# Gated cross-attention and FFN on one core: other orders at the start and in the last three attention pairs, four places for V

## What is computed

```python
q = (layernorm(x) @ Wq)          # 32 heads
k, v = ctx @ Wk, ctx @ Wv        # 8 heads, each used by 4 query heads
q, k = rope(q), rope(k)          # cos/sin rows gathered by position_ids
p = softmax(where(mask == 0, -1e9, q @ k.T / sqrt(128)))
x = x + tanh(g_xattn) * ((p @ v) @ Wo)
x12 = layernorm(x) @ w12.T + b12
x = x + tanh(g_ffn) * ((silu(x12[..., :512]) * x12[..., 512:]) @ w3.T + b3)
```

## Time and profile before

| | |
|---|---|
| median of 3 runs | 682.74 us (681.73 to 683.15) |
| the profiled execution | 682.45 us, of which the span (first to last instruction) is 680.6 us |
| PE busy | 663.5 us, 97% of the span, 3352 matmuls |
| PE weight loads busy | 555.4 us, 82% |
| DVE, POOL, ACT busy | 485.0, 385.3, 321.9 us |
| mean granted TensorE clock | 0.997 of full |
| chain that ended last | PE 86%, DVE 5%, POOL 3%, ACT 2% |

### The profile page before, as it was taken

One profiled execution on the slowest core, in us unless ns is written; L12 is line 12 of the kernel. 1 busy time (PEld: TensorE's weight loads), 2 busy tenths in 40 slices (PEclk: granted clock), 3 DMA queues, 4 the chain that ended last, 5 costly groups with the idle time before them and its releaser, 6 DMA issues.

```text
span 680.6 us, 11325 instructions
## 1 busy us (share of the span) xinstructions
PE 663.5 (97%) x3352; PEld 555.4 (82%) x3352; DVE 485.0 (71%) x1223; ACT 321.9 (47%) x903; POOL 385.3 (57%) x323
## 2 busy tenths in 40 slices
PE   7999999999999999999999999999999998999998
PEld 6777888778888888888888888888888886778886
DVE  2788575887777777777777777777777776774433
ACT  4343722554544545445445454454454536766210
POOL 5546766886556666665566666655666655531000
PEclk8999999999999999999999999999999999999999
DMA  9977894232122131213212121221210042000002
GB/s 304 311 242 232 272 309 155 90 97 93 58 83 93 35 105 33 92 31 108 91 32 94 47 92 31 93 70 69 77 33 31 32 155 79 0 1 1 1 31 93
DMA packets 62157, 66.34 MB, mean 97 GB/s; under 512 B 5920, under 2 KB 43808, under 8 KB 62112
## 3 DMA queue, kind: packets, MB, share of 16 engines
q1 hardware_dynamic: 60688, 64.77, 29.4%
q0 software_dynamic: 384, 1.05, 0.5%
q10 hardware_dynamic: 1040, 0.00, 0.1%
HBM read 46.93 MB, written 18.87 MB: 97 GB/s over the span
## 4 chain that ended last, share of the span: by engine, by line
PE 86%; DVE 5%; POOL 3%; ACT 2%; issue 2%; DMA 1%; SPq 0%; DVEq 0%; POOLq 0%; ACTq 0%
PE f_bank L459 10%; PE f_bank L461 10%; PE f_bank L460 10%; PE o_bank L459 9%; PE o_bank L461 9%; PE o_bank L460 9%; PE s_banks L583 6%; PE t_bank L465 4%; PE pv_bank L459 3%; PE pv_bank L461 3%; PE pv_bank L460 3%; PE s_banks L584 2%; PE t_bank L459 1%; PE s_banks L459 1%; PE t_bank L460 1%
## 5 line engine op out<-in xcount | busy, mean ns | idle before, releaser
L1104 POOL TENSOR_TENSOR prob<-prob,small 128x512 f32<-128x512 f32 x64 | 66.7, 1042 | 139.5 <-DVE small L1345 139.5
L864 ACT ACTIVATE prob<-prob,small 128x128 f32<-128x128 f32 x256 | 99.8, 391 | 81.4 <-DVE small L1335 75.9
L795 ACT ACTIVATE o_hi<-pv_bank 128x512 fp32r<-128x512 f32 x64 | 38.5, 601 | 145.7 <-PE pv_bank L461 145.4
L459 PE MATMUL o_bank<-wo_hi,o_hi 128*128 128x512 f32 x256 | 105.7, 413 | 0.0
L459 PE MATMUL f_bank<-xT_hi,wq_hi 128*128 128x512 f32 x256 | 101.5, 396 | 0.0
L461 PE MATMUL o_bank<-wo_hi,o_lo 128*128 128x512 f32 x256 | 100.5, 393 | 0.0
L1060 POOL TENSOR_TENSOR q_lo<-q,q_hi 128x512 fp32r<-128x512 f32 x64 | 82.8, 1293 | 30.6 <-ACT q_hi L795 30.6
L460 PE MATMUL o_bank<-wo_lo,o_hi 128*128 128x512 f32 x256 | 100.0, 391 | 0.0
L461 PE MATMUL f_bank<-xT_hi,wq_lo 128*128 128x512 f32 x256 | 99.8, 390 | 0.0
L460 PE MATMUL f_bank<-xT_lo,wq_hi 128*128 128x512 f32 x256 | 99.8, 390 | 0.0
L1247 DVE TENSOR_TENSOR t_sin<-f_bank,rope 64x512 f32<-64x512 f32 x128 | 88.2, 689 | 2.8
(11 more groups left out here) (180 smaller groups left out, 1468.7 us busy)
## 6 DMA issues: line engine op xcount, KB each, us to landing
k_scratch<-ks_parts SPq DMA_DIRECT2D x16, 512.0 KB, 3.1
raw<-in_L_xattn_Wq_dram SPq DMA_DIRECT2D x32, 256.0 KB, 2.8
raw<-in_L_xattn_Wo_dram SPq DMA_DIRECT2D x32, 256.0 KB, 2.6
k_parts<-k_scratch SPq DMA_DIRECT2D x16, 512.0 KB, 3.6
v_scratch<-vs_hi SPq DMA_DIRECT2D x16, 256.0 KB, 3.7
v_scratch<-vs_lo SPq DMA_DIRECT2D x16, 256.0 KB, 4.0
v_hi<-v_scratch SPq DMA_DIRECT2D x16, 256.0 KB, 3.9
v_lo<-v_scratch SPq DMA_DIRECT2D x16, 256.0 KB, 4.2
```

Of the source, the lines that this page charges most:

```text
L459: nc.tensor.matmul(dst, st[0], mv_[0], start=start, stop=False)
L864: e = nc.scalar.activation(prob[:, k, h, :], prob[:, k, h, :], ACT.Exp, bias=nmin[k][:, h:h + 1], scale=-1.0, accum_out=psum_row[k][:, h:h ...
L1104: nc.gpsimd.tensor_tensor(prob[:, k], prob[:, k], rrow[k].unsqueeze(2).to_broadcast([128, GH, S]), ALU.mult).then_inc(pool_norm, 1)
```

## The change

1. **Start of PE.** `warm(6)` instead of `warm(2)` behind ctx tile 0, none behind tile 1, `warm(3)` behind tile 3. ctx tile 3 goes ahead of the first K block instead of into it.
2. **Gathers.** POOL issues six of the eight indirect DMAs ahead of its three weight splits, then two (before: four and four).
3. **First K copies.** The ACT copies of the first two K blocks (`k_hi_copy(0)`, `(1)`) stand at stage index 2 and 3, behind the V copy there, instead of at 1 and 2.
4. **V places.** `vs_hi` and `vs_lo` get four places each and take the whole space of q32. `V_SLOT` is 0 to 3 in turn for V blocks 0 to 11, then 2, 3, 2, 3. In return `add_q(0, e)`, which writes q32, waits for all stores of place e % 4.
5. **x normalised sooner.** `x_norms` for tiles 0, 1 and 2, 3 at stage index 11 and 13, before 15 and 16.
6. **Last three pairs.** On PE `out_proj(c-1, 0)` stands between the two scores of a pair; FFN tiles move by a place; in the last pair `out_proj(3, 7, 0)` stands ahead of `pv(3, 7, 1)`. `h_tile(3)` goes to a half of s_banks. The lists of ACT, POOL and DVE follow.

```diff
-        vs_hi = place("vs_hi", [128, 2, 512], F32R, at["q32"] + 8192)
-        vs_lo = place("vs_lo", [128, 2, 512], F32R, at["q32"] + 12288)
+        vs_hi = place("vs_hi", [128, 4, 512], F32R, at["q32"])
+        vs_lo = place("vs_lo", [128, 4, 512], F32R, at["q32"] + 8192)
...
+        V_SLOT = [vi % 4 if vi < 12 else 2 + vi % 2 for vi in range(16)]
...
             warm(WARM)
             tile("ctx", 0)
-            warm(2)
+            warm(6)
             tile("ctx", 1)
-            warm(2)
             tile("ctx", 2)
+            tile("ctx", 3)
+            warm(3)
             tiles_done(tile_of("ctx", 1))
-            k_block(0, 0, 0, 3)
+            k_block(0, 0, 0)
             tiles_done(tile_of("ctx", 3))
...
+            out_proj(3, 6, 0)
             scores(3, 7, 1)
-            out_proj(3, 6, 0)
-            ffn_tile(5)
+            ffn_tile(6)
             prob_transpose(3, 7, 0)
             out_proj(3, 6, 1)
             pv(3, 7, 0)
             prob_transpose(3, 7, 1)
-            ffn_tile(6)
             ffn_tile(7)
+            out_proj(3, 7, 0)
             pv(3, 7, 1)
-            out_proj(3, 7, 0)
...
-                if vi >= 2:
-                    act.wait_ge(v_stored[vi % 2], 32 * (vi // 2))
+                slot = V_SLOT[vi]
+                if vi >= 4:
+                    act.wait_ge(v_stored[slot], v_stores(slot, vi))
...
-                if i and STAGE[i - 1][0] == "K":
+                if i in (2, 3) or i > 3 and STAGE[i - 1][0] == "K":
                     k_hi_copy(kk)
                     kk += 1
...
-                if i in (15, 16, 18, 19):
-                    b = {15: 0, 16: 2, 18: 4, 19: 6}[i]
+                if i in (11, 13, 18, 19):
+                    b = {11: 0, 13: 2, 18: 4, 19: 6}[i]
...
+            pT_hi_copy(3, 5, 0)
             exps(3, 5, 1)
-            pT_hi_copy(3, 5, 0)
             ffn_tile_copy(0)
-            q_hi_copy(3, 6, 1)
             o_hi_copy(3, 5, 0)
             pT_hi_copy(3, 5, 1)
             ffn_tile_copy(1)
             o_hi_copy(3, 5, 1)
-
+            q_hi_copy(3, 6, 1)
...
-                    if e == 4:
-
-                        pool.wait_ge(v_stored[0], 32 * 8)
-                        pool.wait_ge(v_stored[1], 32 * 8)
+
+                    pool.wait_ge(v_stored[e % 4], v_stores(e % 4, 16))
...
-            for b in range(4):
+            for b in range(6):
                 gather(b)
             for s in range(3, 6):
                 first_chunk(s)
-            for b in range(4, 8):
+            for b in range(6, 8):
                 gather(b)
...
             ffn_tile_lo(0)
+            ffn_tile_lo(1)
             q_lo_split(3, 6, 1)
-            ffn_tile_lo(1)
+            norm(3, 6, 0)
             q_lo_split(3, 7, 0)
...
             o_lo_split(3, 6, 1)
-            mask_first(3, 7, 1)
+            h_stats(3)
             recip(3, 7, 0)
-            mask_rest(3, 7, 1)
-            h_stats(3)
+            add_out(3, 6, 0)
+            mask_scores(3, 7, 1)
+            pT_lo_split(3, 7, 0)
             inv_std_begin(0, 4, NEWTON_OPS)
             newton_step(0, 4, NEWTON_OPS, 0)
-            pT_lo_split(3, 7, 0)
             recip(3, 7, 1)
-            add_out(3, 6, 0)
+            add_out(3, 6, 1)
+            o_lo_split(3, 7, 0)
+            pT_lo_split(3, 7, 1)
             for step in range(1, NEWTON):
                 newton_step(0, 4, NEWTON_OPS, step)
             shifts(0, 4)
```

More of the change, by code:

```diff
@@ L172, in build @@
         k_stored = [sem(f"k_stored{i}") for i in range(2)]
-        v_stored = [sem(f"v_stored{i}") for i in range(2)]
+        v_stored = [sem(f"v_stored{i}") for i in range(4)]
         k_loaded = [sem(f"k_loaded{i}") for i in range(2)]
@@ L233, in pool_split, with v_stores @@
             return s + 1 - len(V_CHUNKS)
+        V_SLOT = [vi % 4 if vi < 12 else 2 + vi % 2 for vi in range(16)]
+        def v_stores(slot, before):
+            return 32 * V_SLOT[:before].count(slot)
         def wk_parts(group):
@@ L390, in _ @@
                 if i == 22:
-                    sp.wait_ge(v_stored[0], 32 * 4)
-                    sp.wait_ge(v_stored[1], 32 * 4)
+                    for slot in range(4):
+                        sp.wait_ge(v_stored[slot], v_stores(slot, 8))
                     load_v(0, 0)
@@ L398, in _ @@
                 sp.wait_ge(k_stored[half], 16 * KBLOCKS // 2)
-                sp.wait_ge(v_stored[half], 32 * 8)
+            for slot in range(4):
+                sp.wait_ge(v_stored[slot], v_stores(slot, 16))
             def load_chunk(o, G):
@@ L486, in tile, with k_block @@
                 mm.then_inc(pe_tile, 1)
-            def k_block(r, kk, part=None, between=None):
+            def k_block(r, kk, part=None):
                 group, half = K_ORDER[kk]
@@ L501, in k_block @@
                     w = slice(k * 128, (k + 1) * 128)
-                    if between is not None and k == 2:
-                        tile("ctx", between)
                     mm = three(dst, (hi[:, w], lo[:, w]), (cT_hi[:, k, tk], cT_lo[:, k, tk]), k == 0, k == KT - 1)
@@ L678, in h_tile @@
                 elif b == 3:
[L679 to L680 removed]
+                    pe.wait_ge(dve_mask, 8 * KVH)
                 elif b < 6:
@@ L717, in down @@
                 mm.then_inc(pe_down, 1)
+            out_proj(3, 4, 0)
             scores(3, 5, 1)
-            out_proj(3, 4, 0)
             ffn_tile(0)
-            ffn_tile(1)
             prob_transpose(3, 5, 0)
@@ L728, in _ @@
             scores(3, 6, 0)
+            ffn_tile(1)
             ffn_tile(2)
             pv(3, 5, 1)
+            out_proj(3, 5, 0)
             scores(3, 6, 1)
-            out_proj(3, 5, 0)
             ffn_tile(3)
@@ L1008, in _ @@
             pT_hi_copy(3, 6, 1)
+            ffn_tile_copy(4)
             o_hi_copy(3, 6, 1)
+            q_hi_copy(3, 7, 1)
             exps(3, 7, 0)
-            ffn_tile_copy(4)
+            ffn_tile_copy(5)
+            pT_hi_copy(3, 7, 0)
             exps(3, 7, 1)
-            pT_hi_copy(3, 7, 0)
-            ffn_tile_copy(5)
+            ffn_tile_copy(6)
             o_hi_copy(3, 7, 0)
             pT_hi_copy(3, 7, 1)
+            ffn_tile_copy(7)
             h_norm(0)
             h_norm(1)
+            h_norm(2)
             o_hi_copy(3, 7, 1)
-            ffn_tile_copy(6)
-            ffn_tile_copy(7)
-            h_norm(2)
             h_norm(3)
@@ L1173, in _ @@
             ffn_tile_lo(0)
+            ffn_tile_lo(1)
             q_lo_split(3, 6, 1)
-            ffn_tile_lo(1)
+            norm(3, 6, 0)
             q_lo_split(3, 7, 0)
-            norm(3, 6, 0)
             ffn_tile_lo(2)
             norm(3, 6, 1)
+            ffn_tile_lo(3)
+            ffn_tile_lo(4)
             q_lo_split(3, 7, 1)
-            ffn_tile_lo(3)
             norm(3, 7, 0)
-            ffn_tile_lo(4)
+            ffn_tile_lo(5)
             norm(3, 7, 1)
-            for t in range(5, FFN_TILES):
+            for t in range(6, FFN_TILES):
                 ffn_tile_lo(t)
@@ L1273, in v_lo_split @@
                 dve.wait_ge(act_vhi, vi + 1)
-                lo(vs_lo[:, vi % 2, :], v_bank[vi % 2][:, :], vs_hi[:, vi % 2, :], dve_vlo)
+                lo(vs_lo[:, V_SLOT[vi], :], v_bank[vi % 2][:, :], vs_hi[:, V_SLOT[vi], :], dve_vlo)
             def first_chunk(s):
```

33 lines of the change are left out of this document (15 added, 18 removed).

## The result

The changed kernel takes **674.44 us** (median of 4 runs, 674.06 to 674.53) where the kernel before took 682.48 (4 runs, 681.73 to 683.15): ratio 0.9881, 95% interval [0.9867, 0.9895]. The forecast was 674.2, range 671.8 to 677.9. The profiled execution took 674.48 us, its span is 672.7. PE is now busy for 661.8 us (98% of the span), and holds 90% of the chain that ended last (before 86%).

The account below looks back on a forecast made before the run. PE bounds the kernel (busy 444.4 of 450 us in the loop), so only the two ends move: 6.0 (first part) + 2.6 (last pairs) = 8.6 off 682.45 is 673.85; median 674.1, taken as 674.2, range 671.8 to 677.9.

Parts of the forecast that it names:

- Start: First K block: rope tiles start at about 15.05 instead of 16.36, ended by the fourth gather's landing; 1.3 us gained.
- V blocks 1 to 4: PE's stalls before V2, V3 and V4 go, with slow restarts; 2.3 us gained, bounds 1.0 and 2.4.
- The stall before V4: PE idle 0.72 us because V2's copy waited for V0's store; four places remove it, within the 2.3 us.
- K(2, 0): K block waiting for weight chunk 6: 0.35 to 0.4 of its 0.97 us stall stays; 0.6 us gained.
- x tiles: PE's 1.36 us wait for ACT's x_norms goes, with restart and a late second tile; 1.8 us gained.
- Price of the places: add_q(0, 2) and (0, 3) wait for stores of V14 and V15: cost 0, bound a loss of 1 us.
- Last three pairs: Waits before scores, 3.2 us, go; softmax chain and layernorm come next; 2.6 us gained, bounds 0 and 4.8.
- the walk through the pairs: Three last pairs followed through five queues with old durations: transpose of (3, 7, 1) at 594.7 instead of 596.66.
- The FFN part: PE stream behind out_proj(3, 7, 1) to the end: same instructions and same length as before.
- new lower clock: Rival, chance 0.05: the 1.2 us gather wait ahead of V0 lowers the clock, costing 1.7 us: 675.9.
- The Q split behind two FFN splits: Rival, chance 0.03: POOL's late Q split stretches pairs from 12 to 16 us: 688.5; scores waiting for q_lo would show it.
- The collision of DVE and POOL: Last layernorm's Newton steps: a POOL FFN split among the last six adds 1.3 us; without it the gain is 3.4.

Follow-up runs that it names:

- e_old_start: The changed kernel with PE's old start order (warm 2 and 2, ctx tile 3 inside the first K block): 674.79 us.
- e_places_only: The kernel before with the four V places alone: 680.66 us.
- e_best: Changed kernel; POOL holds FFN tile 7's split for DVE's last layernorm step, two normalisations on DVE, FFN tiles 1, 4, 7 ahead of second probability transposes: 671.71 us.

## Why the prediction was right, point by point

- **Start, 1.3 forecast, 1.68 measured.** The end that it named, the landing of the fourth gather, is the one: rope tile 1 at 15.09 against 15.05. The sum was short because rope tile 0 was now transposed during the wait (13.85), so V0 follows one tile later, not two. Of the 1.68, 0.3 to 0.6 is the order of PE at the faster pace; the rest is mostly the pace of the first K block, as shown above.
- **V blocks 1 to 4, 2.3 forecast, 2.28 measured: right, on a reason that holds but is not the only one.** "Their cause is the ACT queue: the V0 copy stands behind K copy 0": from the old start the two orders remove the stalls with no help from PE's start (e_old_start against e_places_only, 1.24 us). What the prediction did not see is that the new start does most of it too (0.77 from V0 to V4), by letting ACT's weight copies, POOL's splits and its sum come sooner; it costed this part for PE alone. So with the new start either order can be undone by itself and no stall comes back before V2 and V3.
- **The places.** The stall before V4 was taken as 0.72 us with its restart. For the kernel before this is right (places alone gave 1.2 us to the first scores). As a statement on the change it was far too small: without the places the other parts won next to nothing, since the store's time hardly moved with PE. The prediction priced each stall as it stood in the old trace, and did not ask how long a wait becomes when PE comes 3.5 us earlier.
- **K(2, 0), 0.6 forecast, 0.84 measured.** POOL's split of weight chunk 6 ended at 40.04, 0.6 us sooner than worked out, just where PE wanted it (V5 at 37.29 and 2.72). The new place of the K copies, costed as harmless, is a gain here: with the old one it waits 0.64 us.
- **x tiles, 1.8 forecast, 1.49 at the tiles and 1.8 up to the block behind (K(4, 0) at 62.82, before 69.41).** Right, and confirmed by undoing it.
- **Price of the places, 0.** Right: from the x tiles to the first scores nothing was lost.
- **Last three pairs, 2.6 forecast, 1.65 measured.** The mechanism was right (the waits before scores go, waits for POOL's normalisation and for ACT's xnorm take their place). The size was off in the walk through the pairs: on before's clock it had the second transposes of (3, 7) at 594.7, and they came at 589.02 + 6.53 = 595.55. The waits themselves were shorter than worked out (0.41, 0.23, 0.66 and 0.68 us, 1.98 together, for 2.5), so 1.4 us more than forecast lie in the work between them. One FFN tile more than before stands ahead of that transpose, 0.45 us. Scores (3, 6, 1) and (3, 7, 1) each came some 0.27 us late, held by POOL's Q split behind two FFN splits: it ended at 570.69 and 582.80, and the scores began at 570.79 and 582.91, so that the output product ahead of them takes 3.07 us where 2.8 is usual. The rest, some 0.4 us, is not traced. Then the layernorm ended at 593.26 + 6.53 = 599.8, later than the 597.9 to 598.9 of the forecast: 0.85 from the transposes, and 0.98 from the one step that POOL held. POOL's Q split of (3, 6, 1), and PE's first matmul of the scores:

```profile
569.39 1.30 POOL L1072 TENSOR_TENSOR q_lo<-q,q_hi 128x512 fp32r<-128x512 f32 x1
```

```profile
570.79 0.36 PE L591 MATMUL s_banks<-k_parts,q_hi 128*128 128x256 f32 x1 [0.15 <-issue]
```

- **The FFN part, the same length forecast.** It took 72.31 us from out_proj(3, 7, 1) to the last result instead of 72.10.
- **Rivals.** No new lower clock appeared in the changed kernel. The Q split behind two FFN splits did hold scores (3, 6, 1) and (3, 7, 1), which the prediction had named as a sign of being wrong, but by 0.27 us each and not by the 4 us per pair of that rival; in e_best, where an FFN tile stands further ahead, the output products before these scores take 2.80 and 2.79 us. The collision of DVE and POOL cost its one us. The sum had most of that already: 602.75 lies near the later end of 602.0 to 603.0, 2.6 us of gain where 3.4 stood without the collision. So the shortfall of the pairs is mainly the 0.85 us from the transposes.
- **The total is closer than its terms.** The first part gave 6.59 us for 6.0, the last pairs 1.65 for 2.6, and the FFN part took 0.2: the errors have both signs. The profiled executions differ by 7.97 us for 8.6 forecast. The median is nearer, 674.44 for 674.2, because the forecast started from a median before of 682.74 which further executions put at 682.48. That part is luck.

## What to carry to other kernels

A wait read from a trace has the length that it has at that pace: before taking it as the price of a missing buffer, ask which time ends it, and whether that time moves with the rest. Here one DMA store behind others in SP's queue hardly moved, so the same two places cost 0.7 us of waiting before and 3.5, with the lower clock behind it, once PE was faster. Where a queue is strict, follow a late operand back over all engines to the first instruction that waited, and ask which of the other edits frees it too. Undoing one edit of a finished change showed nothing here, because the other had freed the same copies; only undoing both, and each from the old side, told what they are worth. And once the large waits are gone, small operations of DVE beside a POOL tensor operation are worth a look: one semaphore that kept them apart gave 1.1 us.
